# An attention layer over a graph: the place of a register load and of the softmax turns in the edge loop

## What is computed

```python
q_att = jnp.einsum('nhd,rhde->rnhe', q, relation_att)
v_msg = jnp.einsum('nhd,rhde->rnhe', v, relation_msg)
attn_score = jnp.sum(q_att[etype, col_idx] * k[row_idx], axis=-1)
score = attn_score * (relation_pri[etype] / SQRT_DK)
m = segment_max(score, col_idx)
ex = jnp.exp(score - m[col_idx])
denom = segment_sum(ex, col_idx)
agg = segment_sum((ex / denom[col_idx])[..., None] * v_msg[etype, row_idx], col_idx)
```

## Time and profile before

| | |
|---|---|
| median of 3 runs | 2159.93 us (2157.82 to 2164.44) |
| profiled execution | 2155.21 us, span of the core 2153.9 us |
| mean granted TensorE clock | 0.963 |
| TensorE matmul busy | 1885.7 us, 88% |
| VectorE busy | 1637.1 us, 76% |
| ScalarE busy | 1460.9 us, 68% |
| GpSimd busy | 1189.2 us, 55% |

### The profile page before, as it was taken

How to read it: one execution, slowest core, us unless ns; L and a number is a source line. 1 busy time by engine, 2 the same in 40 slices (tenths; PEclk the granted TensorE clock), 3 DMA queues, 4 the chain that set the end, 5 groups by cost and what they waited for, 6 DMA issues and landing times.

```text
span 2153.9 us, 37341 instructions
## 1 busy us (share of the span) xinstructions
PE 1885.7 (88%) x10336; PEld 1428.7 (66%) x10336; DVE 1637.1 (76%) x3979; ACT 1460.9 (68%) x4926; POOL 1189.2 (55%) x1207
## 2 busy tenths in 40 slices
PE   6999998998689999998999999999999873926999
PEld 6865555555567777777778777777777752614666
DVE  8757776654589999989989999998999985873111
ACT  7855555554378888888889887888888863831221
POOL 0033334432776777777777776777777703502554
PEclk9999999999899999999999999999999996956999
DMA  7958888999999999989999999999999917671221
GB/s 237 324 188 324 316 321 278 370 363 369 299 319 300 315 313 304 311 295 300 307 296 320 317 311 300 303 306 302 314 306 319 311 45 231 193 269 50 75 76 43
DMA packets 271461, 583.71 MB, mean 271 GB/s; under 512 B 45078, under 2 KB 185962, under 8 KB 264600
## 3 DMA queue, kind: packets, MB, share of 16 engines
q0 software_dynamic: 93936, 384.51, 51.4%
q1 hardware_dynamic: 177320, 196.82, 28.2%
HBM read 407.81 MB, written 176.99 MB: 272 GB/s over the span
## 4 chain that ended last, share of the span: by engine, by line
PE 54%; DVE 23%; issue 11%; DVEq 3%; POOL 3%; ACT 3%; DMA 3%; SPq 0%; POOLq 0%; ACTq 0%
PE bank L985 9%; PE bank L804 7%; PE bank L969 6%; PE bank L1143 4%; PE bank L1154 4%; PE bank L783 4%; PE bank L865 4%; DVE arena L1972 3%; DVE arena L2065 3%; PE bank L950 3%; POOL arena L2378 3%; DVE arena L2029 3%; PE bank L650 2%; PE bank L706 2%; PE bank L694 2%
## 5 line engine op out<-in xcount | busy, mean ns | idle before, releaser
L2378 POOL DMA_INDIRECT arena<-table,arena x880 | 874.8, 994 | 327.5 <-issue 253.5
L1355 ACT ACTIVATE arena<-arena 128x64 f32<-128x64 f32 x3432 | 839.7, 340 | 0.0
L985 PE MATMUL bank<-arena 128*128 128x260 f32 x1760 | 436.0, 391 | 45.2 <-DVE arena L2065 42.1
L985 PEld LDWEIGHTS bank<-arena 128*128 128x128 f32 x1760 | 321.0, 191 | 122.2 <-issue 74.3
L1972 DVE TENSOR_TENSOR arena<-bank,arena 128x512 f32<-128x512 f32 x440 | 300.4, 685 | 71.9 <-PE bank L969 45.1
L969 PE MATMUL bank<-arena 128*128 128x256 bf16 x2640 | 335.2, 275 | 7.5 <-DVE arena L1972 7.5
L969 PEld LDWEIGHTS bank<-arena 128*128 128x128 bf16 x2640 | 258.3, 99 | 64.0 <-DVE arena L1972 8.9
L1982 DVE TENSOR_REDUCE arena<-arena 128x16 f32<-128x1024 f32 x220 | 268.0, 1218 | 20.7 <-DVE arena L1972 0.9
L804 PE MATMUL bank<-arena 64*128 64x512 f32 x832 | 207.2, 613 | 17.0 <-DVE arena L1717 11.9
L1237 ACT COPY arena<-bank 128x512 f32<-128x512 f32 x260 | 149.1, 595 | 81.7 <-PE bank L804 81.0
L2065 DVE TENSOR_TENSOR arena<-arena,bank 128x260 f32 x440 | 184.3, 419 | 7.6 <-PE bank L985 2.4
(11 more groups left out here) (324 smaller groups left out, 2975.5 us busy)
## 6 DMA issues: line engine op xcount, KB each, us to landing
arena<-q_parts SPq DMA_DIRECT2D x440, 192.0 KB
arena<-chunk_rel SPq DMA_DIRECT2D x220, 128.0 KB, 5.4
arena<-table,arena POOLq DMA_INDIRECT x880, 5.1
node_rows<-arena SPq DMA_DIRECT2D x24, 512.0 KB, 6.3
xl_and_sum<-arena SPq DMA_DIRECT2D x3, 3072.0 KB, 18.2
arena<-in_x SPq DMA_DIRECT2D x12, 512.0 KB, 7.7
xn<-arena SPq DMA_DIRECT2D x12, 512.0 KB, 8.0
xT<-arena SPq DMA_DIRECT2D x12, 512.0 KB, 8.1
```

The lines of the kernel that those rows point to most:

```text
L985: ins = TE.matmul(bank[b][:, 0:AW], lhsT=so[p % 2][:, c % 2, j, :], rhs=values_of(c, j), start=j == 0, stop=j == HALF - 1)
L1355: ins = A.activation(seg, seg, ACT.Copy, scale=rows[:, C + h:C + h + 1])
L2378: G.indirect_dma_start(rows_of_pair(p, i % 2 * HALF + j), None, d_tab_rows[0:N * R, :], bass.IndirectOffsetOnAxis(ap=idxE[:, g, j, c:c + 1 ...
```

## The change

It has two parts. On VectorE `load_places` moves from behind `edge_targets` to behind the second `add_chunk` of the same step, ahead of the second product. The softmax chain is moved: on VectorE `row_tops` goes from ahead of the score to behind the first mix half-step of the same step, and `chain_rows` from behind that half-step to the next step, between products and score; on TensorE `turn_scores` goes behind the first mix half-step, `turn_ends` into the next step behind `expand`, and `turn_weights` behind the second mix half-step. `turn_carry` and `shift_rows` stay. Nothing is computed differently, and no instruction is added or removed.

```diff
@@ -1027,18 +1027,18 @@
             g, at_ = divmod(p, PG)
             if p < NPAIR:
                 expand(p)
+            if group_ready(p - 1) >= 0:
+                turn_ends(group_ready(p - 1))
+            next(work, None)
             if group_ready(p) >= 0:
                 turn_scores(group_ready(p))
-            next(work, None)
             if p >= SUM_LAG:
                 scatter(p - SUM_LAG)
-            if group_ready(p) >= 0:
-                turn_ends(group_ready(p))
             if group_ready(p - 1) >= 0:
                 turn_carry(group_ready(p - 1))
+            next(work, None)
             if group_ready(p - 2) >= 0:
                 turn_weights(group_ready(p - 2))
-            next(work, None)
         for _ in work:
             pass
         TE.wait_ge(ex_put, SG)
@@ -2078,10 +2078,12 @@
             for i in range(2):
                 if a >= 0:
                     add_chunk(2 * a + i)
+                if i == 1 and 2 * (a + 1) % PLACES == 0 and 0 <= a + 1 < NPAIR:
+                    load_places(2 * (a + 1) // PLACES)
                 if p < NPAIR:
                     product(p, i)
-            if group_ready(p) >= 0:
-                row_tops(group_ready(p))
+            if group_ready(p - 1) >= 0:
+                chain_rows(group_ready(p - 1))
             if p < NPAIR:
                 score(p)
             if p + 2 < NPAIR:
@@ -2090,11 +2092,9 @@
                 edge_targets(p - TARGET_LAG)
             if SHARED + WEIGH_LAG <= p < NPAIR + WEIGH_LAG:
                 weigh(p - WEIGH_LAG)
-            if 2 * (a + 1) % PLACES == 0 and 0 <= a + 1 < NPAIR:
-                load_places(2 * (a + 1) // PLACES)
             next(work, None)
             if group_ready(p) >= 0:
-                chain_rows(group_ready(p))
+                row_tops(group_ready(p))
             next(work, None)
             if group_ready(p - 1) >= 0:
                 shift_rows(group_ready(p - 1))
```

## The result

| | us | against before |
|---|---|---|
| before | 2159.49 (2155.94 to 2164.44) | |
| after | 2219.3 (2217.35 to 2224.01) | 1.0276, 95% interval 1.0259 to 1.0293 |
| forecast | 2203 (2172 to 2232) | |

The change makes the kernel 59.8 us slower, where +43 was forecast. The profiled execution after took 2217.35 us; its span is 2215.9 us, 62.0 more than before, and the mean granted clock is 0.954.

The account below looks back on a forecast made before the run. VectorE was taken as the closer bound, TensorE nearly level. Holes net 19.8 us minus 5.0 swallowed gave 14.8 us a period, times 2.89 periods +42.8 us: 2198.0 profiled, median 2203 us, range 2172 to 2232.

Parts of the forecast that it names:

- 52 holes: VectorE, second product: each load before the last product leaves a 1.25 us hole, 18 per 72-step period.
- the load's old exposure: VectorE, load's old place behind `edge_targets`: 0.15 us a load already exposed, 2.7 us a period, subtracted from the holes.
- Both rivals about its size: Second product's hole: 0 if load stays hidden (2152 us, chance 0.08); 1.95 upper bound (2230 us, sharing chance 0.12).
- The last three loads: Behind the last product, where VectorE has only additions, targets and weighing: claimed to cost nothing.
- the table: VectorE's waits by group step where heavy mix steps begin: sum 14.2 us a period before, 10.45 after.
- max(0, 3.3 - E): VectorE's wait per mix in us, E being its extras (softmax parts, loads, holes) in the three heavy steps.
- the move is worth nothing by itself: Softmax steps moved without the holes: the waits sum to 14.2 us a period before and after.
- the waits swallow: VectorE's waits for TensorE take up 5.0 us a period of the holes: 3.75 by the table plus 1.2 added.
- the second rival: TensorE, held at `turn_carry` in step 1, starts heavy mixes late: 1 us for each of 27 groups, 2230 us; chance 0.12.
- new waits on `expand` in steps 2 and 3: VectorE, after step 1: deciding sign of TensorE falling behind; the forecast is wrong if they exceed those of before.

Follow-up runs that it names:

- the late `turn_carry`: Whole change with `turn_carry` moved behind `expand` of the next step, against the kernel before, on two slower chips: 2479.29 us (1.0129) and 2474.8 us (1.0125).
- e9_exp_first: Kernel before with ScalarE's exponentials of a group put ahead of its weighing instructions in the same step, against the kernel before: 2433.74 us, 0.9961.
- e6_load_only: Only `load_places` moved behind the second addition, softmax order unchanged, against the kernel before (2448.07 us on that chip): 2461.79 us, 1.0047.
- the fourth run: Only the load moved, `load_places` written twice but just one of each two ran, against the kernel before (2426.32 us): 2431.42 us, 1.0028.

## Why the prediction was right, and where it was off

The sign, the range and the main term held; the amount was 17 us short. The forecast's own sum, set against the three traces of 2160-us chips (us; the loop is from the first product of step 0 to that of step 219, 1191.5 us before):

| term | forecast | load alone | whole change |
|---|---|---|---|
| 52 holes | +65.0 | +64.3 | +62.4 |
| the load's old exposure and the rest of the loop | -7.8 | -9.8 | -7.9 |
| waits for `expand` | -14.4 | -16.7 | **+3.7** |
| waits for gathers | 0 | -0.4 | -1.6 |
| sum in the loop | +42.8 | +37.4 | +56.6 |
| steps behind the last product | 0 | +4.7 | +3.6 |
| ahead of the loop and in the closing stage | 0 | +4.5 | +1.8 |
| span | +42.8 | +46.6 | +62.0 |

The second line of the measured columns is what is left of the loop's growth.

- **The hole** was right in place and size: 1.18 us for 1.25. Both rivals about its size fall (0 and 1.95). The load starts 0.1 us behind the second addition's address, for which the sequencer has waited. The Trainium skill (Advanced Engine Details and Errata, Engine Queue Depths) gives VectorE a queue of 8 instructions; with room for that many, and no wait before it, the load could have started ahead of the first product. The trace shows no such lead, and since a wait stood in the way it says nothing against the depth. That the place of the load sets its price is shown by the load alone, +2.05%.
- **The last three loads**, costed at nothing, were not free. Each opens a hole of 1.47 us, longer than in the loop, since no product stands between the additions; the steps behind the last product grow by 3.6 us, against 4.4 us of holes. VectorE's timeline of the kernel after, one of the three:

```profile
1820.37 0.69 DVE L2029 TENSOR_TENSOR arena<-arena 128x512 f32<-128x512 f32 x1 [1.47 <-issue]
```

- **Luck in the table.** Its sum for the kernel before, 14.2 us, is near the trace's 15.5, but its rows are not: for the begins at 5, 6, 7, 0, 1, 2, 3, 4 the trace has 2.6, 0.4, 1.6, 0.8, 2.9, 2.4, 1.8 and 3.0 us, where the table has 2.65, 0.3, 0, 0, 2.15, 3.3, 3.15 and 2.65. Its base of 3.3 us also takes in the 0.67 us at 1090.38, which belong to step 100, ahead of the heavy steps that begin at 101; without them it is 2.6.
- **What failed** is "the move is worth nothing by itself", and with it "the waits swallow" 5.0 us a period. The table of max(0, 3.3 - E) takes it that TensorE goes on working while VectorE does its extras. That holds for the load alone, in the sum: by the table its waits are 9.8 us a period (14.2 before), by the trace 11.8 (15.5 before). For the whole change the table says 10.45 and the trace 17.9. By the step of the group (p modulo 8) at which a mix's three heavy steps begin, with the time of the nine steps from that step's first product, and the waits for `expand` in them (us):

| begins at | from step | nine steps: before | load alone | whole change | waits, load alone: table | trace | waits, whole change: table | trace |
|---|---|---|---|---|---|---|---|---|
| 5 | 101 | 49.5 | 51.5 | 51.8 | 1.55 | 1.4 | 1.55 | 1.7 |
| 6 | 110 | 46.9 | 48.4 | 49.7 | 0.3 | 0.2 | 2.0 | 1.4 |
| 7 | 119 | 48.7 | 49.9 | 50.2 | 0 | 1.5 | 0 | 1.9 |
| 0 | 128 | 49.7 | 51.6 | 50.0 | 0 | 0.8 | 0 | 0.8 |
| 1 | 137 | 50.6 | 53.3 | 56.7 | 1.05 | 2.2 | 0 | **4.0** |
| 2 | 146 | 48.4 | 50.4 | 52.3 | 3.3 | 2.2 | 3.3 | **3.9** |
| 3 | 155 | 49.4 | 50.8 | 52.1 | 2.05 | 1.9 | 2.05 | 2.3 |
| 4 | 164 | 49.7 | 50.1 | 51.1 | 1.55 | 1.7 | 1.55 | 1.9 |
| sum | | 393.0 | 406.1 | 413.8 | 9.8 | 11.9 | 10.45 | 17.9 |

By the table the move adds 0.65 us of waits to the load alone, by the traces 6.0. Most of the difference, 4.5 us, lies in two rows: where the heavy steps begin at step 1 of a group (1.8 us more instead of 1.05 less), and where they begin at step 2, just behind it (1.7 more instead of none). In times the move adds 7.7 us to the load alone. Two of its terms only shift 1.7 us over the boundary between two rows, since `chain_rows` has moved from step 136 to step 137: without that shift the rows that begin at 0 and 1 grow by 0.1 and 1.7 us, and the one that begins at 2 by 1.9. The timeline of step 137 in the kernel after (start us, us, engine, line; in brackets the idle time before it):

```profile
1318.82 0.38 PE L999 MATMUL bank<-arena 128*1 128x128 f32 x2 [2.54 <-DVE arena L1992]
...
1318.99 0.68 DVE L1972 TENSOR_TENSOR arena<-bank,arena 128x512 f32<-128x512 f32 x1
1319.03 1.90 PE L941 MATMUL bank<-arena 128*128 128x256 f32 x8
...
1320.77 1.89 PE L950 MATMUL bank<-arena 128*128 128x256 f32 x8
...
1321.20 0.69 DVE L1972 TENSOR_TENSOR arena<-bank,arena 128x512 f32<-128x512 f32 x1 [1.18 <-issue]
...
1328.05 0.60 ACT L1329 ACTIVATE arena<-bank 128x512 f32<-128x512 f32 x1 [2.67 <-PE bank L950]
...
1330.80 0.33 PE L1012 MATMUL bank<-arena 128*128 128x128 f32 x1 [1.04 <-ACT arena L1334]
...
1331.90 0.69 DVE L1972 TENSOR_TENSOR arena<-bank,arena 128x512 f32<-128x512 f32 x1 [1.08 <-PE bank L969]
...
1338.45 0.70 DVE L1972 TENSOR_TENSOR arena<-bank,arena 128x512 f32<-128x512 f32 x1 [2.35 <-PE bank L969]
```

And the same step with the load alone:

```profile
1308.70 0.38 PE L999 MATMUL bank<-arena 128*1 128x128 f32 x2 [0.18 <-DVE arena L1992]
...
1310.25 1.90 PE L941 MATMUL bank<-arena 128*128 128x256 f32 x8
...
1311.98 1.89 PE L950 MATMUL bank<-arena 128*128 128x256 f32 x8
...
1314.08 0.68 DVE L1972 TENSOR_TENSOR arena<-bank,arena 128x512 f32<-128x512 f32 x1
1314.31 2.05 PE L985 MATMUL bank<-arena 128*128 128x260 f32 x8 [0.44 <-DVE arena L2065]
...
1316.28 0.69 DVE L1972 TENSOR_TENSOR arena<-bank,arena 128x512 f32<-128x512 f32 x1 [1.18 <-issue]
```

With the load alone TensorE has asked for the ends at 1308.70, early in VectorE's step 136, and both mix products (941, 950) are done at 1313.87, before VectorE's first product of step 137 at 1314.08. In the kernel after `turn_ends` stands ahead of the mix, and `row_tops`, on which it waits, is now the last thing of VectorE's step. So TensorE stands idle for 2.54 us ahead of its heaviest work, and ends it at 1322.66, 3.7 us behind that product. Its lead is gone when the heavy steps begin, and VectorE, which has its hole, `chain_rows` and `shift_rows` in the same step, pays once more two and three steps later, 1.08 and 2.35 us. In the load alone the first of these two waits is absent and the second is 1.83 us. The first of them has one more link: `expand` stands behind `turn_weights`, where TensorE waits 1.04 us for ScalarE's exponentials, and ScalarE comes to them late: it stood idle for 2.67 us until the late mix product (950) had ended, and went on at 1328.05, 1.4 us into VectorE's step 138. With the load alone it goes on 0.4 us ahead of that step, and this matmul of `turn_weights` starts without a wait. VectorE's extras no longer take the place of its waits; TensorE waits through them.

In the growth of the row that begins at 2 something else takes part, for which the forecast has no term: TensorE's clock. The timeline of step 145 in the kernel after, and the window that follows (columns as in the earlier trace rows; the clock is the number ahead of the last two):

```profile
1370.91 0.38 PE L1005 MATMUL bank<-arena 1*128 1x4 f32 x2 [2.12 <-DVE arena L2013]
...
1373.35 2.90 PE L941 MATMUL bank<-arena 128*128 128x256 f32 x8
```

```profile
1372.00:1375.40 3.40, 3.40 (x13) 2.67 (x12) 3.29 (x10) 0.00 (x0) 2.72 (x3) 0.50 0.86 287
```

TensorE has stood in `turn_carry` for 2.12 us; then the granted clock is 0.50 (1.2 of 2.4 GHz) from 1372.0 to 1375.4, and a mix product takes 2.90 us there that takes 1.89 at full clock. Two and three steps later products wait 0.80 and 0.66 us for `expand`, which the load alone, at full clock in the same step, does not have. The granted clock of the whole loop is 0.99 before, 0.98 with the load alone and 0.97 after: it is at 0.50 for 20, 37 and 54 us. In the kernel after, 7 such stretches begin within 2 us of the end of a hold of 2.1 to 2.3 us in `turn_carry`, a hold that the load alone does not have. The 17 us more at half clock are 8.5 us of TensorE's work, beside the 19 us by which the loops of the load alone and of the whole change differ. What it costs apart from the holds no run shows.

This is the second rival's mechanism, "TensorE falls behind in step 1", at a smaller price than its 27 us and with the hold first at `turn_ends`, not only at `turn_carry`. The forecast named new waits on `expand` in steps 2 and 3 as its sign; they came a step later than that, in steps 3 and 4 of the group (139 and 140, the last two rows of the first timeline), where the kernel before waits 0.53 and 2.39 us. That the move costs something is shown four times on chips of the second kind (+0.4 to +0.7%, 10 to 18 us), and the 16.5 us between the load alone and the whole change on 2160-us chips has the same size. That the cause there is the hold before the mix, and the lost clock behind the holds, is read from the traces, not shown by an experiment: the move alone and the late `turn_carry` were not run on such a chip, and a kernel with `turn_ends` left in its old step was not tried.

## What to carry to other kernels

The register load on VectorE's sequencer, 1.83 us long, opened a hole of its length less the engine work handed over before it started: 0.75 us behind a score, 1.18 behind the additions, 1.47 where no product stood between them. So it belongs behind a long run of instructions without a wait, and not between an addition whose address is only just known and the work that could cover it. What a hole costs is another question: 52 of them, 64.3 us, cost 42 us where the kernel takes 2160 us. An estimate in which one engine's extra work takes the place of its waits for another holds only while the other can go on; before moving a two-way exchange (turn, scan, turn) look at what stands behind each half of it. The traces suggest keeping the half that waits behind the waiting engine's heavy work and not ahead of it; no run tested that. `e9_exp_first`, 0.9961 of the kernel before, is the one version here that beat it, on one chip of the second kind; it was not tried on the first.

## What was not expected of the hardware

The price of the same edit depends on the chip: the load alone costs 2.05% where the kernel takes 2160 us and 0.3 to 0.5% where it takes 2426 or 2448, though the holes of 1.18 us are in both traces. The latter chips lose their time in waits of another sort. The timeline of the load alone on one of them (`e6_load_only`; "remote" stands where the profile names no releaser of this core):

```profile
1106.41 1.90 PE L916 MATMUL bank<-arena 128*128 128x256 f32 x8
...
1113.23 0.69 DVE L1972 TENSOR_TENSOR arena<-bank,arena 128x512 f32<-128x512 f32 x1 [3.90 <-remote]
1113.36 0.39 ACT L1304 ACTIVATE arena<-bank 128x256 f32<-128x256 f32 x1 [5.59 <-remote]
...
1114.00 0.95 POOL L2378 DMA_INDIRECT arena<-table,arena  x1 [2.50 <-remote]
```

ScalarE's instruction at 1113.36 needs the matmul of line 916, which had ended at 1108.3; VectorE, ScalarE and GpSimd go on within a microsecond of each other. Stretches of over 0.7 us in which TensorE, VectorE and ScalarE all stand still are absent between 600 and 1700 us of the three traces of 2160-us chips, and there are 11 to 24 of them (17 to 47 us) in each of the others. That is a small part of the 262 to 295 us between the kernels before on the two kinds. The granted clock is lower there too, 0.91 to 0.93 in all these runs (0.963 in the first trace of the kernel before). The view of line 1972 of the fourth run has most of the difference ahead of the products:

```profile
  remote: 196.0, 80
  issue: 63.2, 50
  PE bank L969: 17.4, 24
```

By the program a product waits for `expand` or for gathered rows alone, and these traces lack the landing times of the gathers, so late rows are the likely reason; that is not shown. A wait put down to "remote" can cover a hole of the sequencer's as one for `expand` can, and 196 us of them are there; that this is why the load is cheaper on those chips fits, and was not tested. What makes these chips slower is open.
